# Involution stage: four row tiles for its kernel maps, sums and last convolution as 64x64 products

## The chip, the core and the metric

The kernel runs on one core of one Trainium2 chip. The engines are TensorE (PE, matrix products into PSUM; its weight loads are shown apart as PEld), VectorE (DVE), ScalarE (ACT), GpSimd (POOL) and SyncE (SP, which here only starts transfers). They run side by side and meet through semaphores. The metric is the device time of one execution in microseconds (us).

## What is computed

Eight blocks are applied in turn to 8 images of 64 channels and 16x16 pixels, in 32-bit floats. The change touches the seventh, the involution; its input is layer-normalised over the channels and its result is added to x:

```python
def conv1x1(x, w, b):
    return jnp.einsum('oc,bchw->bohw', w, x) + b[None, :, None, None]

def involution(x, w_red, b_red, w_span, b_span):
    kern = conv1x1(jax.nn.relu(conv1x1(x, w_red, b_red)), w_span, b_span)
    patches = extract_patches(x)        # the nine shifted copies, 3x3, zero padded
    return jnp.einsum('bkhw,bckhw->bchw', kern, patches)
x = dwconv3x3(x, w_in, b_in)            # depthwise, 3x3
x = involution(x, w_red, b_red, w_span, b_span)
x = dwconv3x3(x, w_out, b_out)          # depthwise, 3x3
```

`w_red` takes 64 channels to 16, `w_span` these to 9: one map per tap, the same for all channels.

## The kernel before

X is [128, 1024]: partitions are two halves of 64 channels (images 0-3 and 4-7), columns four images of 256 pixels. A half h of the columns is a pair of images (HC = 512 columns). Work is cut by h; the program of each engine is written out in order, and engines wait for each other by counting semaphores. Each block of the network is a Block of the program, at whose ends all engines meet.

In the involution's block (from L1636) the order is this. The layer norm (`ln_pe`, `ln_act`, `ln_dve`) ends in YP, a padded copy. The first depthwise convolution runs for h=0 on PE (nine products with diagonal matrices DGI of 128x128, L1674), placed in padded ZP by ACT (L1701), and for h=1 on DVE (L1723 to L1729). For each h, PE reduces ZP to 2x16 rows (L1678), ACT writes them into R with Relu (L1704), and row 32 of R is a row of ones that carries the bias of the maps. Then PE makes nine maps (L1684), each spread over the 64 channels of both halves, in PSUM banks 0 to 3 in turn. DVE multiplies each by the shifted window of ZP (L1740) and adds it to ACC (L1745), the last sum going to padded OP (L1743); a map's bank is free when its product is made (`k_used`). The last convolution of h=0 is nine products on PE (L1691). Of h=1, PE takes PTAPS = 4 taps and DVE the other five (L1747, L1749), which DVE adds to X (L1753); L1756 and L1758 add PE's parts from PSUM. DGI is made in the block before, by POOL. The next block begins with the layer norm of the last one (L153).

A product of 32-bit floats stands in the trace as two MATMUL records and two LDWEIGHTS records, one for each pass.

Of the kernel before, what the change touches and what calls it, by code (L numbers as in the profile page):

```python
# [11 lines left out]
ALU = mybir.AluOpType  # L12
# [47 lines left out]
    [("dwi", 9), ("dbi", 1), ("red", 32), ("bred", 1), ("span", 9 * P), ("dwo", 9), ("dbo", 1)],  # L60
# [12 lines left out]
def build(nc, x_dram, packs, idx_dram, out_dram):  # L73
    with ExitStack() as ctx:
# [1561 lines left out]
        with ExitStack() as sctx, nc.Block() as block:  # L1636
# [4 lines left out]
            M = sb("M7", [P, 2, HC], F32, sctx)  # L1641
            ACC = sb("ACC7", [P, COLS], F32, sctx)
            y_pad, pads, ones_set, z_ps, r_ps, r_in, k_ps, k_used, o_ready, o_ps = (sem("s7_" + n) for n in (
                "y_pad", "pads", "ones_set", "z_ps", "r_ps", "r_in", "k_ps", "k_used", "o_ready", "o_ps"))
            z_in = [sem(f"s7_z_in{h}") for h in range(2)]
            PTAPS = 4
            WROWS = PITCH + H
            WIN = sb("WIN", [P, WROWS, W], F32, sctx)

# [7 lines left out]
            @block.gpsimd  # L1657
            def _(pool):
                pool.memset(YP[:, :, :], 0.0).then_inc(y_pad, 1)
                for b in (ZP, OP):  # L1660
                    pool.memset(b[:, :, :], 0.0).then_inc(pads, 1)

                after_pool(pool, pool.memset(R[:, :], 0.0))
                pool.memset(R[32:33, :], 1.0).then_inc(ones_set, 1)

            @block.tensor
            def _(pe):
# [8 lines left out]
                for h in range(2):  # L1676
                    pe.wait_ge(z_in[h], 1)
                    pe.matmul(bank(6 + h)[0:32, :], wt("red"), pair(ZP, h, 2, 2), start=True, stop=True).then_inc(r_ps, 1)  # L1678
                    pe.wait_ge(r_in, h + 1)
                    for k in range(9):  # L1680
                        n = 9 * h + k
                        if n >= 4:
                            pe.wait_ge(k_used, n - 3)
                        pe.matmul(bank(n % 4), wt("span", k * P, P), R[:, h * HC:(h + 1) * HC],  # L1684
                                  start=True, stop=True).then_inc(k_ps, 1)

                for h in range(2):
                    pe.wait_ge(o_ready, h + 1)
                    taps = 9 if h == 0 else PTAPS
                    for m in range(taps):  # L1690
                        mm = pe.matmul(bank(4 + h), DGI[:, 9 + m, :], pair(OP, h, 1 + m // 3, 1 + m % 3), start=(m == 0), stop=(m == taps - 1))  # L1691
                    mm.then_inc(o_ps, 1)

            @block.scalar
            def _(act):
# [3 lines left out]
                act.wait_ge(ones_set, 1)  # L1699
                act.wait_ge(z_ps, 1)  # L1700
                act.activation(pair(ZP, 0, 2, 2), images(bank(4)), ACT.Identity, bias=wt("dbi")).then_inc(z_in[0], 1)  # L1701
                for h in range(2):
                    act.wait_ge(r_ps, h + 1)
                    act.activation(R[0:32, h * HC:(h + 1) * HC], bank(6 + h)[0:32, :], ACT.Relu, bias=wt("bred", 0, 1, 0, 32)).then_inc(r_in, 1)  # L1704


# [6 lines left out]
            def _(dve):  # L1713
# [19 lines left out]
                for h in range(2):  # L1733
                    dve.wait_ge(z_in[h], 1)
                    for k in range(9):
                        n = 9 * h + k
                        c = slice(h * HC, (h + 1) * HC)
                        dve.wait_ge(k_ps, n + 1)
                        o = ACC[:, c] if k == 0 else M[:, n % 2, :]
                        dve.tensor_tensor(images(o), images(bank(n % 4)), pair(ZP, h, 1 + k // 3, 1 + k % 3), ALU.mult).then_inc(k_used, 1)  # L1740
                        dve.wait_ge(k_used, n + 1)
                        if k == 8:
                            dve.tensor_tensor(pair(OP, h, 2, 2), images(ACC[:, c]), images(M[:, n % 2, :]), ALU.add).then_inc(o_ready, 1)  # L1743
                        elif k:
# [432 lines left out]
```

## Time and profile before

| | us |
|---|---|
| median of 3 runs | 609.9 (608.07 to 611.87) |
| the profiled execution | 609.04 |
| its span | 607.3 |
| PE, DVE, ACT, POOL busy | 513.8, 365.2, 293.1, 142.8 |
| involution block, from L153 at 454.11 to the last write of X at 505.03 | 50.92 |
| of it, from the first map at 472.25 | 32.78 |

The span runs from the first to the last instruction of the profiled execution; its own time has 1.7 us more around it. In a row of the timeline "x6" means six instructions merged into one line, from the start of the first to the end of the last; the bracket behind it is the time that the engine stood idle before, and what ended it. Sizes of PE rows are weight rows * columns, then the moving operand.

### The profile page before, as it was taken

To read this page: it belongs to the slowest core of one execution; us is meant where nothing else is said; L and a number is where in the kernel's file an instruction comes from. 1 tells how busy PE (TensorE), PEld (TensorE's weight loads), DVE (VectorE), ACT (ScalarE), POOL (GpSimd) and SP (SyncE) were. 2 spreads that over 40 slices of the span, in tenths; PEclk is the share of its full clock that TensorE was granted. 3 is DMA by queue.
4 is the path that set the end of the run, shared out by engine and by line. 5 is a ranking of instruction groups with operands and counts; after the bars stand their busy time and mean duration, and the time that the engine had idled before them with its cause. 6 is when DMAs were issued, how large, how long until landed. Compare 5 with 4: busy or idle time off the path is not lost. (4 is left out here: it accounts for less than half of the span.)

```text
span 607.3 us, 11742 instructions
## 1 busy us (share of the span) xinstructions
PE 513.8 (85%) x4973; PEld 263.1 (43%) x4973; DVE 365.2 (60%) x587; ACT 293.1 (48%) x393; POOL 142.8 (24%) x136
## 2 busy tenths in 40 slices
PE   3899989878998996788888788749997898999994
PEld 1334324543224966777687442313323334433231
DVE  2377994673554559878869257561437796633534
ACT  2573225255531159999998356635551102344230
POOL 8070000010011005888878300042002002000000
PEclk9999999998998999899899889868999999999998
DMA  7000000020000035455452000110002000000000
GB/s 251 1 2 2 2 1 1 1 102 0 1 16 16 2 104 206 160 184 195 176 177 74 1 19 0 49 42 0 1 13 101 0 1 1 1 0 1 3 15 17
DMA packets 7988, 29.42 MB, mean 48 GB/s; under 512 B 864, under 2 KB 2176, under 8 KB 7552
## 3 DMA queue, kind: packets, MB, share of 16 engines
q1 hardware_dynamic: 7936, 28.67, 14.1%
q8 instruction: 39, 0.64, 0.4%
q14 instruction: 13, 0.11, 0.1%
HBM read 28.00 MB, written 0.67 MB: 47 GB/s over the span
## 5 line engine op out<-in xcount | busy, mean ns | idle before, releaser
L1073 PE MATMUL PS<-GX,OH 128*128 128x64 f16 x2304 | 73.6, 195 | 19.1 <-DVE OH L1237 9.5
L1073 PEld LDWEIGHTS PS<-GX,OH 128*128 128x128 f16 x2304 | 71.0, 99 | 24.1 <-issue 12.7
L1162 ACT ACTIVATE DIST<-BC,wbuf 128x2048 f16<-128x2048 f16 x24 | 48.0, 2000 | 3.1 <-DMA BC<-idx_dram 1.4
L1969 DVE TENSOR_SCALAR HID<-PS,wbuf 128x512 f32<-128x512 f32 x32 | 23.8, 750 | 41.6 <-PE PS L1862 41.6
L1165 ACT ACTIVATE OH<-DIST 128x2048 f16<-128x2048 f16 x24 | 45.9, 1911 | 0.8
L1237 DVE TENSOR_SCALAR OH<-BC,wbuf 128x2048 f16<-128x2048 f16 x48 | 43.8, 935 | 2.6 <-DMA BC<-idx_dram 2.6
L1008 POOL TENSOR_TENSOR V<-SQ 128x512 f32<-128x512 f32 x18 | 27.9, 1547 | 57.5 <-DVE SQ L1248 56.7
L1908 ACT ACTIVATE HID<-PS,wbuf 128x512 f32<-128x512 f32 x32 | 22.0, 687 | 37.1 <-PE PS L1862 37.1
L692 DVE SCALAR_TENSOR_TENSOR D<-QKVP,wbuf,D 128x1024 f32<-128x1024 f32 x27 | 34.6, 1281 | 7.7 <-ACT D L592 6.9
L181 ACT ACTIVATE SQ<-PS 128x512 f32<-128x512 f32 x16 | 9.6, 597 | 60.9 <-PE PS L153 52.7
L153 PE MATMUL PS<-X,wconst 128*128 128x512 f32 x32 | 19.2, 731 | 22.9 <-DMA wconst<-pack_dram 8.6
L1858 PE MATMUL PS<-Y,wbuf 64*128 64x512 f32 x128 | 36.6, 615 | 2.3 <-DVE HID L1969 2.3
L423 PE MATMUL PS<-T,DG 128*32 128x512 f32 x336 | 37.1, 594 | 0.0
L1011 POOL TENSOR_TENSOR VAL<-V 128x256 f32<-128x256 f32 x36 | 35.9, 997 | 2.8
L1248 DVE TENSOR_TENSOR SQ<-PS,WC 128x512 f32<-128x512 f32 x36 | 23.1, 683 | 14.7 <-PE PS L1073 13.3
L921 DVE TENSOR_TENSOR HS<-PS,HID 128x512 f32<-128x512 f32 x32 | 20.6, 685 | 18.5 <-PE PS L806 18.4
L1870 PE MATMUL PS<-HID,wbuf 128*64 128x512 f32 x128 | 30.8, 604 | 0.0
L1008 POOL TENSOR_TENSOR V<-SD 128x512 f32<-128x512 f32 x18 | 26.7, 1485 | 4.8 <-DVE SD L1248 3.8
L873 ACT ACTIVATE HID<-PS,wbuf 128x512 f32<-128x512 f32 x32 | 20.1, 682 | 13.2 <-PE PS L797 13.1
L1248 DVE TENSOR_TENSOR SD<-PS,WC 128x512 f32<-128x512 f32 x36 | 23.1, 681 | 5.6 <-PE PS L1073 3.3
L1628 DVE TENSOR_TENSOR H2W<-H,WB 128x512 f32<-128x512 f32 x16 | 10.5, 689 | 24.7 <-ACT H L1569 12.5
L592 ACT ACTIVATE D<-PS,wbuf 128x512 f32<-128x512 f32 x12 | 8.3, 689 | 28.6 <-PE PS L423 28.6
(309 smaller groups left out, 931.0 us busy)
## 6 DMA issues: line engine op xcount, KB each, us to landing
BC<-idx_dram SPq DMA_DIRECT2D x36, 512.0 KB, 4.2
wbuf<-pack_dram SPq DMA_DIRECT2D x1, 1913.0 KB, 10.2
wbuf<-pack_dram SPq DMA_DIRECT2D x1, 1656.0 KB, 6.8
wbuf<-pack_dram SPq DMA_DIRECT2D x1, 1494.5 KB, 6.1
wbuf<-pack_dram SPq DMA_DIRECT2D x1, 820.0 KB, 11.7
wbuf<-pack_dram SPq DMA_DIRECT2D x1, 732.0 KB, 4.2
wbuf<-pack_dram SPq DMA_DIRECT2D x1, 602.5 KB, 3.4
X<-x_dram SPq DMA_DIRECT2D x2, 256.0 KB, 4.2
```

The source lines that it names most:

```text
L423: mm = pe.matmul(bank(DBANK[t % 2] + n)[32 * q:32 * q + 32, :], DG[:, (2 * j + hf) * NBLK + i, :], src, start=(i == blocks[0]), stop=(i == ...
L692: ins = dve.scalar_tensor_tensor(out=d, in0=window(QKVP[j], dy, dx), scalar=wt("dw5", j * 25 + 5 * dy + dx, 1), in1=d, op0=ALU.mult, op1=A ...
L1008: after_pool(pool, pool.tensor_tensor(V1[:, :, :, :], U[s % 2][:, :, 0:2, :], U[s % 2][:, :, 2:4, :], ALU.add))
L1011: pool.tensor_tensor(VAL[:, (s // 8) % 2, :, s % 8, :], V1[:, :, 0, :], V1[:, :, 1, :], ALU.add).then_inc(val_ready, 1)
L1073: mm = pe.matmul(o, OH[:, s % NOH, qh, t * P:(t + 1) * P], src, start=(qh == 0 and part == 0), stop=(qh == 1 and part == 1))
L1162: after_act(act, act.activation(DIST[:, :], BC[:, s % NBC, :], ACT.Abs, bias=wt("negq1")))
L1165: act.activation(OH[:, s % NOH, 1, :], DIST[:, :], ACT.Relu, bias=1.0, scale=-1.0).then_inc(scalar_oh, 1)
L1237: ins = dve.tensor_scalar(OH[:, s % NOH, qh, :], BC[:, s % NBC, :], wt("qidx", qh, 1), None, ALU.is_equal)
L1248: ins = dve.tensor_tensor(o, src, w, ALU.mult)
L1858: pe.matmul(bank(2 + (n + bh) % 4), wt("w1_3", e * FH3 + m * P, P, r, r + C), Y[r:r + C, bp * HC:(bp + 1) * HC], start=True, stop=False, t ...
L1870: pe.matmul(bank(bp)[C * bh:C * bh + C, :], wt("w2_3", (2 * e + m) * C, C), HID[:, (n + i) % 8, :], start=(e == 0 and m == 0), stop=False) ...
L1969: dve.tensor_scalar(HID[:, n % 8, :], bank(2 + n % 4), wt("b1_3", 2 * e + m, 1), 0.0, ALU.add, ALU.max).then_inc(hid_in_v, 1)
```

## The change

The work of the involution is cut by u, the first or second image of a pair, with both pairs side by side, n = 9u + k. R now holds four copies of the reduced rows (four products of 32 columns in four column tiles), and the weights `span` stand four times too, so that map n uses row tile n % 4 and bank n % 4. The bias of the maps has columns of its own, `bspan`. ACT evicts every map to KM (six buffers), DVE only multiplies (six buffers M), and PE sums the nine products of a u with unit matrices of 64x64: rows from one partition half g, output partitions by pair h, so each M buffer gives four products of 256 columns into two banks. `place` on ACT writes a sum from two banks to OP. The last convolution uses 64x64 blocks of DGI in the same four tiles and brings the images back to their places; DVE adds each u to X.

```diff
-    [("dwi", 9), ("dbi", 1), ("red", 32), ("bred", 1), ("span", 9 * P), ("dwo", 9), ("dbo", 1)],
+    [("dwi", 9), ("dbi", 1), ("red", 32), ("bred", 1), ("span", 9 * P), ("bspan", 9), ("dwo", 9), ("dbo", 1)],
...
-            M = sb("M7", [P, 2, HC], F32, sctx)
-            ACC = sb("ACC7", [P, COLS], F32, sctx)
-            y_pad, pads, ones_set, z_ps, r_ps, r_in, k_ps, k_used, o_ready, o_ps = (sem("s7_" + n) for n in (
-                "y_pad", "pads", "ones_set", "z_ps", "r_ps", "r_in", "k_ps", "k_used", "o_ready", "o_ps"))
+            NK, NM = 6, 6
+            KM = sb("KM7", [P, NK, HC], F32, sctx)
+            M = sb("M7", [P, NM, HC], F32, sctx)
+            y_pad, pads, z_ps, r_ps, r_in, k_ps, k_in, m_ready, m_used, o_in, o_ps = (sem("s7_" + n) for n in (
+                "y_pad", "pads", "z_ps", "r_ps", "r_in", "k_ps", "k_in", "m_ready", "m_used", "o_in", "o_ps"))
             z_in = [sem(f"s7_z_in{h}") for h in range(2)]
-            PTAPS = 4
+            NP = 18
+            ABANK, OBANK = (4, 6), (4, 0)
...
+            def of_pairs(pad, u, dy, dx):
+                base = min(dy, 2)
+                at = u * PITCH + dy - base
+                v = pad[:, base:base + 4 * PITCH, dx:dx + W].rearrange("p (h r) w -> p h r w", h=2)
+                return v[:, :, at:at + H, :]
+            def two_banks(n):
+                return PS[:, n * 512:(n + 2) * 512].rearrange("p (k c) -> p k c", k=2)[:, :, 0:PIX]
...
-                after_pool(pool, pool.memset(R[:, :], 0.0))
-                pool.memset(R[32:33, :], 1.0).then_inc(ones_set, 1)
...
-                for h in range(2):
+                for h in (1, 0):
                     pe.wait_ge(z_in[h], 1)
-                    pe.matmul(bank(6 + h)[0:32, :], wt("red"), pair(ZP, h, 2, 2), start=True, stop=True).then_inc(r_ps, 1)
-                    pe.wait_ge(r_in, h + 1)
-                    for k in range(9):
-                        n = 9 * h + k
-                        if n >= 4:
-                            pe.wait_ge(k_used, n - 3)
-                        pe.matmul(bank(n % 4), wt("span", k * P, P), R[:, h * HC:(h + 1) * HC],
-                                  start=True, stop=True).then_inc(k_ps, 1)
-                for h in range(2):
-                    pe.wait_ge(o_ready, h + 1)
-                    taps = 9 if h == 0 else PTAPS
-                    for m in range(taps):
-                        mm = pe.matmul(bank(4 + h), DGI[:, 9 + m, :], pair(OP, h, 1 + m // 3, 1 + m % 3), start=(m == 0), stop=(m == taps - 1))
-                    mm.then_inc(o_ps, 1)
+                    for q in range(4):
+                        mm = pe.matmul(bank(6 + h)[32 * q:32 * q + 32, :], wt("red"), pair(ZP, h, 2, 2), start=True, stop=True,
+                                       tile_position=(0, 32 * q))
+                    mm.then_inc(r_ps, 1)
+                def maps(i):
+                    for q in range(min(4, NP - 4 * i)):
+                        n, r = 4 * i + q, 32 * q
+                        u, k = n // 9, n % 9
+                        if i:
+                            pe.wait_ge(k_in, n - 3)
+                        rhs = R[r:r + 32, :].rearrange("p (h v x) -> p h v x", h=2, v=2)[:, :, u, :]
+                        pe.matmul(bank(q), wt("span", k * P, P, r, r + 32), rhs, start=True, stop=True, tile_position=(r, 0)).then_inc(k_ps, 1)
+                def add(n):
+                    u, k = n // 9, n % 9
+                    pe.wait_ge(m_ready, n + 1)
+                    for h in range(2):
+                        for g in range(2):
+                            a = C * g
+                            mm = pe.matmul(bank(ABANK[u] + g, PIX)[C * h:C * h + C, :], wt("ident", a, C, a, a + C),
+                                           M[a:a + C, n % NM, h * PIX:(h + 1) * PIX], start=(k == 0), stop=(k == 8), tile_position=(a, C * h))
+                    mm.then_inc(m_used, 1)
+                def out_tap(u, m):
+                    if m == 0:
+                        pe.wait_ge(o_in, u + 1)
+                    for g in range(2):
+                        for h in range(2):
+                            a = C * h
+                            r0 = (2 * g + u) * PITCH + 1 + m // 3
+                            mm = pe.matmul(bank(OBANK[u] + h, PIX)[C * g:C * g + C, :], DGI[a:a + C, 9 + m, a:a + C],
+                                           OP[a:a + C, r0:r0 + H, 1 + m % 3:1 + m % 3 + W], start=(m == 0), stop=(m == 8), tile_position=(a, C * g))
+                    if m == 8:
+                        mm.then_inc(o_ps, 1)
+                pe.wait_ge(r_in, 2)
+                maps(0)
+                maps(1)
+                for n in range(4):
+                    add(n)
+                maps(2)
+                for n in range(4, 8):
+                    add(n)
+                maps(3)
+                for n in range(8, 12):
+                    add(n)
+                maps(4)
+                taps = {12: (0,), 13: (1,), 14: (2, 3), 15: (4,), 16: (5,), 17: (6, 7, 8)}
+                for n in range(12, NP):
+                    add(n)
+                    for m in taps[n]:
+                        out_tap(0, m)
+                for m in range(9):
+                    out_tap(1, m)
...
-                act.wait_ge(ones_set, 1)
                 act.wait_ge(z_ps, 1)
                 act.activation(pair(ZP, 0, 2, 2), images(bank(4)), ACT.Identity, bias=wt("dbi")).then_inc(z_in[0], 1)
-                for h in range(2):
-                    act.wait_ge(r_ps, h + 1)
-                    act.activation(R[0:32, h * HC:(h + 1) * HC], bank(6 + h)[0:32, :], ACT.Relu, bias=wt("bred", 0, 1, 0, 32)).then_inc(r_in, 1)
+                for i, h in enumerate((1, 0)):
+                    act.wait_ge(r_ps, i + 1)
+                    act.activation(R[:, h * HC:(h + 1) * HC], bank(6 + h), ACT.Relu, bias=wt("bred")).then_inc(r_in, 1)
+                def place(u):
+                    act.wait_ge(m_used, 9 * u + 9)
+                    act.activation(of_pairs(OP, u, 2, 2), two_banks(ABANK[u]).rearrange("p k (r w) -> p k r w", w=W), ACT.Copy).then_inc(o_in, 1)
+                for n in range(NP):
+                    act.wait_ge(k_ps, n + 1)
+                    if n >= NK:
+                        act.wait_ge(m_ready, n - NK + 1)
+                    act.activation(KM[:, n % NK, :], bank(n % 4), ACT.Identity, bias=wt("bspan", n % 9, 1)).then_inc(k_in, 1)
+                    if n == 13:
+                        place(0)
+                place(1)
...
-                for h in range(2):
-                    dve.wait_ge(z_in[h], 1)
-                    for k in range(9):
-                        n = 9 * h + k
-                        c = slice(h * HC, (h + 1) * HC)
-                        dve.wait_ge(k_ps, n + 1)
-                        o = ACC[:, c] if k == 0 else M[:, n % 2, :]
-                        dve.tensor_tensor(images(o), images(bank(n % 4)), pair(ZP, h, 1 + k // 3, 1 + k % 3), ALU.mult).then_inc(k_used, 1)
-                        dve.wait_ge(k_used, n + 1)
-                        if k == 8:
-                            dve.tensor_tensor(pair(OP, h, 2, 2), images(ACC[:, c]), images(M[:, n % 2, :]), ALU.add).then_inc(o_ready, 1)
-                        elif k:
-                            after(dve, dve.tensor_tensor(ACC[:, c], ACC[:, c], M[:, n % 2, :], ALU.add))
-                dve.wait_ge(o_ready, 2)
-                after(dve, dve.tensor_scalar(WIN[:, :, :], window(OP, PTAPS), wt("dwo", PTAPS, 1), wt("dbo"), ALU.mult, ALU.add))
-                for m in range(PTAPS + 1, 9):
-                    after(dve, dve.scalar_tensor_tensor(out=WIN[:, :, :], in0=window(OP, m), scalar=wt("dwo", m, 1), in1=WIN[:, :, :],
-                                                        op0=ALU.mult, op1=ALU.add))
-                for i in range(2):
-                    x = X[:, HC + i * PIX:HC + (i + 1) * PIX].rearrange("p (r w) -> p r w", w=W)
-                    ins = dve.tensor_tensor(x, x, WIN[:, i * PITCH:i * PITCH + H, :], ALU.add)
-                after(dve, ins)
-                dve.wait_ge(o_ps, 1)
-                dve.scalar_tensor_tensor(out=X[:, 0:HC], in0=bank(4), scalar=wt("dbo"), in1=X[:, 0:HC], op0=ALU.add, op1=ALU.add)
-                dve.wait_ge(o_ps, 2)
-                dve.tensor_tensor(X[:, HC:COLS], bank(5), X[:, HC:COLS], ALU.add)
+                dve.wait_ge(z_in[0], 1)
+                for n in range(NP):
+                    u, k = n // 9, n % 9
+                    dve.wait_ge(k_in, n + 1)
+                    if n >= NM:
+                        dve.wait_ge(m_used, n - NM + 1)
+                    if n == 0:
+                        dve.wait_ge(z_in[1], 1)
+                    maps = KM[:, n % NK, :].rearrange("p (h r w) -> p h r w", h=2, r=H)
+                    dve.tensor_tensor(M[:, n % NM, :].rearrange("p (h r w) -> p h r w", h=2, r=H), maps,
+                                      of_pairs(ZP, u, 1 + k // 3, 1 + k % 3), ALU.mult).then_inc(m_ready, 1)
+                for u in range(2):
+                    dve.wait_ge(o_ps, u + 1)
+                    x = X[:, :].rearrange("p (h v c) -> p h v c", h=2, v=2)[:, :, u, :]
+                    dve.scalar_tensor_tensor(out=x, in0=two_banks(OBANK[u]), scalar=wt("dbo"), in1=x, op0=ALU.add, op1=ALU.add)
...
+    for q in range(4):
+        for g in range(2):
+            r = 32 * q + 16 * g
+            put("bred", v["L3_conv_b_red"][:, None], r)
+            for k in range(9):
+                put("span", np.broadcast_to(v["L3_conv_w_span"][k][:, None], (16, C)), r, k * P + C * g)
+    rows("bspan", v["L3_conv_b_span"])
```

The next rows list PE's instructions in its order (line, kind, output and inputs, size of the output, how many). First the place where the maps begin, before: the reduction by half (L1678), the maps (L1684), the last convolution (L1691).

```order
L1674 MATMUL PS<-YP,DGI 128x512 x9
L1678 MATMUL PS<-ZP,wbuf 32x512
L1684 MATMUL PS<-R,wbuf 128x512 x9
L1678 MATMUL PS<-ZP,wbuf 32x512
L1684 MATMUL PS<-R,wbuf 128x512 x9
L1691 MATMUL PS<-OP,DGI 128x512 x13
```

The same place in the changed kernel, as far as the fourth group of maps (L1688 reduces, L1700 makes maps, L1709 sums products).

```order
L1683 MATMUL PS<-YP,DGI 128x512 x9
L1688 MATMUL PS<-ZP,wbuf 32x512 x8
L1700 MATMUL PS<-R,wbuf 128x512 x8
L1709 MATMUL PS<-M,wconst 64x256 x16
L1700 MATMUL PS<-R,wbuf 128x512 x4
L1709 MATMUL PS<-M,wconst 64x256 x16
L1700 MATMUL PS<-R,wbuf 128x512 x4
L1709 MATMUL PS<-M,wconst 64x256 x16
L1700 MATMUL PS<-R,wbuf 128x512 x2
```

Maps now come in groups, with the sums of four earlier products between two groups. The end of the stage on PE in the changed kernel follows, from sum 15 on (L1721 is the last convolution, four products to a tap).

```order
L1709 MATMUL PS<-M,wconst 64x256 x4
L1721 MATMUL PS<-OP,DGI 64x256 x4
L1709 MATMUL PS<-M,wconst 64x256 x4
L1721 MATMUL PS<-OP,DGI 64x256 x4
L1709 MATMUL PS<-M,wconst 64x256 x4
L1721 MATMUL PS<-OP,DGI 64x256 x48
```

The 48 are the last three taps of u=0 and all nine of u=1. On DVE the whole stage behind the first convolution was a run of products and additions with taps at its end; here are its first and last rows before (with a line left out between), which the change's two rows below replace.

```order
-L1740 TENSOR_TENSOR ACC<-PS,ZP 128x512
-L1740 TENSOR_TENSOR M<-PS,ZP 128x512
-L1745 TENSOR_TENSOR ACC<-ACC,M 128x512
...
-L1743 TENSOR_TENSOR OP<-ACC,M 128x2x16x16
-L1747 TENSOR_SCALAR WIN<-OP,wbuf 128x544
-L1749 SCALAR_TENSOR_TENSOR WIN<-OP,wbuf,WIN 128x544 x4
-L1753 TENSOR_TENSOR X<-X,WIN 128x256 x2
-L1756 SCALAR_TENSOR_TENSOR X<-PS,wbuf,X 128x512
-L1758 TENSOR_TENSOR X<-PS,X 128x512
...
+L1805 TENSOR_TENSOR M<-KM,ZP 128x512 x18
+L1810 SCALAR_TENSOR_TENSOR X<-PS,wbuf,X 128x2x256 x2
```

Eighteen products and two additions are left on DVE.

## Rows read from the trace of the kernel before

**Rows 1.** Busy time by stretch; columns as in the first line.
```profile
core 0: us, PE busy (x) PEld busy (x) DVE busy (x) ACT busy (x) POOL busy (x), PEclk, DMA share, GB/s
472.25:482.30 10.05, 9.26 (x20) 3.39 (x20) 8.30 (x12) 0.69 (x2) 0.00 (x0) 1.00 0.00 0
482.30:492.60 10.30, 9.16 (x18) 3.11 (x19) 9.83 (x15) 1.02 (x2) 0.00 (x0) 1.00 0.00 0
492.60:504.40 11.80, 11.70 (x27) 4.70 (x25) 10.55 (x17) 0.00 (x0) 0.00 (x0) 1.00 0.01 1
```
**Rows 2.** Timeline, start of the stage: start, length, engine, line, operation [idle before].
```profile
469.66 0.70 ACT L1701 ACTIVATE ZP<-PS,wbuf 128x512 f32<-128x512 f32 x1 [12.05 <-PE PS L1674]
470.42 1.07 PE L1678 MATMUL PS<-ZP,wbuf 128*32 128x512 f32 x2 [0.87 <-ACT ZP L1701]
471.52 0.68 ACT L1704 ACTIVATE R<-PS,wbuf 32x512 f32<-32x512 f32 x1 [1.16 <-PE PS L1678]
472.25 8.31 PE L1684 MATMUL PS<-R,wbuf 128*128 128x512 f32 x18 [0.77 <-ACT R L1704]
473.49 0.69 DVE L1740 TENSOR_TENSOR ACC<-PS,ZP 128x512 f32<-128x512 f32 x1 [4.94 <-PE PS L1684]
```
**Rows 3.** Groups by line in 454 to 515: busy, mean ns | idle before.
```profile
L1740 DVE TENSOR_TENSOR M<-PS,ZP 128x512 f32<-128x512 f32 x16 | 11.1, 691 | 0.7 <-PE PS L1684 0.2
L1745 DVE TENSOR_TENSOR ACC<-ACC,M 128x512 f32<-128x512 f32 x14 | 9.7, 691 | 0.5
L1743 DVE TENSOR_TENSOR OP<-ACC,M 128x512 f32<-128x512 f32 x2 | 1.4, 692 | 0.1
```
**Rows 4.** Timeline, end of the stage on DVE.
```profile
497.42 0.69 DVE L1743 TENSOR_TENSOR OP<-ACC,M 128x512 f32<-128x512 f32 x1
498.15 0.56 DVE L1747 TENSOR_SCALAR WIN<-OP,wbuf 128x544 f32<-128x544 f32 x1
498.75 3.25 DVE L1749 SCALAR_TENSOR_TENSOR WIN<-OP,wbuf,WIN 128x544 f32<-128x544 f32 x4
502.03 0.76 DVE L1753 TENSOR_TENSOR X<-X,WIN 128x256 f32<-128x256 f32 x2
502.83 0.75 DVE L1756 SCALAR_TENSOR_TENSOR X<-PS,wbuf,X 128x512 f32<-128x512 f32 x1
504.34 0.69 DVE L1758 TENSOR_TENSOR X<-PS,X 128x512 f32<-128x512 f32 x1 [0.76 <-PE PS L1691]
```
**Rows 5.** Groups by line in 454 to 515, the last convolution on PE.
```profile
L1691 PE MATMUL PS<-OP,DGI 128*128 128x512 f32 x26 | 11.7, 604 | 0.0
```
**Rows 6.** Timeline of DVE and ACT where six independent operations follow each other.
```profile
427.03 3.70 DVE L1628 TENSOR_TENSOR H2W<-H,WB 128x512 f32<-128x512 f32 x6 [12.24 <-ACT WB L1592]
132.09 3.75 ACT L873 ACTIVATE HID<-PS,wbuf 128x512 f32<-128x512 f32 x6
```
**Rows 7.** Timeline of PE: 256 columns without tiles, then 64x64 tiles; L1533's mean; L1684's min/median/max ns.
```profile
425.26 1.89 PE L1533 MATMUL PS<-WT,SEL 128*128 128x256 f32 x8
116.55 2.81 PE L526 MATMUL PS<-ATT,wbuf 64*64 64x512 f32 x24
L1533 PE MATMUL PS<-WT,SEL 128*128 128x256 f32 x8 | 1.9, 379 | 0.0
L1684 PE MATMUL PS<-R,wbuf x36: 592/593/697, 472.3 to 492.2; 128*128 128x512 f32 x36
```
**Rows 8.** The chain that ended last, in order of time: start, length, what.
```profile
577.36 1.87 PE PS L1870 x8
579.23 1.06 PE PS L1858 x4
580.29 0.22 PE PS L1862 x2
580.50 0.86 PE PS L1858 x4
581.36 0.22 PE PS L1862 x2
581.58 1.87 PE PS L1870 x8
```
**Rows 9.** Busy time by stretch, columns as in rows 1: PE's clock.
```profile
183.40:186.80 3.40, 1.27 (x20) 0.86 (x24) 3.24 (x7) 0.87 (x2) 1.27 (x2) 1.00 0.00 0
186.80:190.20 3.40, 3.40 (x20) 1.28 (x16) 1.29 (x3) 0.00 (x0) 0.00 (x0) 0.51 0.02 5
469.60:473.00 3.40, 1.81 (x4) 0.62 (x5) 0.00 (x0) 1.38 (x2) 0.00 (x0) 1.00 0.00 0
```

More of the change, by code:

```diff
@@ L2135, in pack_weights @@
     diag2("red", v["L3_conv_w_red"].T, 0)
-    put("bred", v["L3_conv_b_red"][:, None], 0)
-    put("bred", v["L3_conv_b_red"][:, None], 16)
-    for k in range(9):
-        a = np.broadcast_to(v["L3_conv_w_span"][k][:, None], (16, C))
-        put("span", a, 0, k * P)
-        put("span", a, 16, k * P + C)
-        put("span", np.broadcast_to(v["L3_conv_b_span"][k:k + 1, None], (1, P)), 32, k * P)
+    for q in range(4):
[5 more added lines that the diff above has]
+    rows("bspan", v["L3_conv_b_span"])
     twice("dwo", v["L3_conv_w_out"].reshape(C, 9))
```

## The prediction, made before the changed kernel was run

> **What bounds the kernel now.** I first read the stretches of the involution stage [rows 1]. The stage's own body lies between 472.25, where the first kernel map is issued, and 505.03 us, where the last addition into X ends. In the three stretches between them DVE is busy 8.30 of 10.05, 9.83 of 10.30 and 10.55 of 11.80 us, ACT 0.69, 1.02 and 0.00, and TensorE runs at its upper level (granted clock 1.00, so 2.4 GHz) throughout. The timeline of the start [rows 2] shows a serial hand-over: ACT places ZP, PE reduces, ACT writes R, PE makes the first map at 472.25, and DVE starts its first product at 473.49. From there DVE is a chain: 18 products and 16 additions (14 + 2), each 691 or 692 ns [rows 3], and since each waits for the one before, two of them follow 0.72 us apart (473.49 and the last OP addition at 497.42: 33 steps of 0.725). Behind it, the timeline of the end [rows 4]: five taps on DVE, two additions, then the two that read PSUM, end 504.34 + 0.69 = 505.03. PE's 26 records at 604 ns [rows 5] lie beside this; they end only just behind DVE (a wait of 0.76). So DVE's chain of 31.5 us sets the stage, PE follows it within 0.8 us, and ACT is free.
>
> **What the change removes and adds.** DVE loses 16 additions, the five taps and three of the four closing steps; it keeps 18 products (now of two SBUF operands) and two closing additions of 0.75 us. ACT gains 18 evictions and 2 placements of OP. PE gains 18 sums, each a quad of 64x64 products with 256 columns, and its last convolution becomes 18 quads of the same shape (all nine taps of all images) where 13 full-array products of 512 columns stood. The maps shrink from 18 full-array products to five groups of up to four row tiles. POOL's memsets of R go; nothing waited for them. The start up to 472.25 stays: the reduction is now issued four times side by side, h=1 first, but h=0 still waits for the same ZP at 470.36.
>
> **Prices.** DVE: H2W's six independent products took 3.70 us, so one is 0.69 long and the next starts (3.70 - 0.69) / 5 = 0.60 later; ACT: six evictions with bias took 3.75 us, so 0.61 [rows 6]. A product is two records. A record of 512 columns takes 0.43 us of the array (four of L1858 on two tiles took 0.86 [rows 8]) and, at 0.59 long [rows 7], is readable about 0.16 later; one of 256 columns takes (1.89 - 0.38) / 7 = 0.216 [rows 7]. Do four 64x64 tiles run together? Yes: 24 records of 512 columns (6 quads of records, one per tile) took 2.81 us, that is (2.81 - 0.59) / 5 = 0.44 per four [rows 7]. No row has 64x64 with 256 columns. Bounds: 2 x 0.216 = 0.43 us for a quad of products if the four still run together, 0.86 if a quad took as long as one of 512 columns. I take 0.43 for the sums and 0.445 for the taps, whose operand is a padded window (11.70 us for 26 records is 0.444 each against 0.43 [rows 5, 8]); the weight loads, the only thing that could stretch a shorter product, did not stretch the 256-column row.
>
> Changing the tiling costs something. In the chain at the end of the program [rows 8] L1858 (64x128 tiles) takes 0.86 us in a row of its own tiling and 1.06 behind L1870 (128x64 tiles); L1870 takes 1.87 where four records' time in sequence, 4 x 0.43, is 1.72. So 0.20 into tiles with 128 columns of weights and 0.15 into tiles with 64, and the new tiling starts only when the old one has streamed out. The Trainium skill (TensorEngine Tiling (Array Packing), Key Properties) says that changing the mode drains TensorE, while other tiles of one mode work in parallel. By that rule every switch here is paid; without it the seven switches behind the first maps would cost nothing and the sum below would be 1.2 us smaller (4 x 0.15 + 3 x 0.20). The row agrees with the rule.
>
> **The new path, step by step** (PE's order: maps 0-3, 4-7, sums 0-3, maps 8-11, sums 4-7, maps 12-15, sums 8-11, maps 16-17, then sums and taps).
> - Maps 0-3 issue at 472.25, are readable at 473.36 (0.10 for the first load, 2 x 0.43, 0.16). ACT evicts them; evictions end at 474.05, 474.65, 475.25, 475.85. Maps 4-7 each wait for one of these (the bank), the last issues at 475.94 and streams to 476.90. This paced group is the one real bubble: DVE's products, 0.60 apart, hide behind it.
> - Sums 0-3: 0.15 + 4 x 0.43 = 1.88, to 478.78. Maps 8-11, all banks free: 0.20 + 0.86 = 1.06, to 479.84. Sums 4-7: 1.88, to 481.74.
> - ACT had waited for maps 8-11 (its eviction 7 ends at 478.3) and starts at 480.04; its evictions end every 0.60, the fourth at 482.5. Map 15 waits for that one, streams to 483.53. From the end of sums 4-7 that is 1.8 us where an unpaced group takes 1.06.
> - Sums 8-11: 1.88, to 485.41. Maps 16-17: 1.06, to 486.47. Then six sums with nine tap quads: 0.15 + 6 x 0.43 + 9 x 0.445 = 6.75, to 493.22; the products are all ready by 488.7 and PE waits for none.
> - Placement 1 follows sum 17 (491.9 + 0.16, 0.69 long: 492.8), just inside this; its cover is the three taps behind sum 17 (1.34 us against 1.0). Nine tap quads: 4.0, to 497.23. Readable at 497.4, DVE's last addition 0.75 long: 498.2; with 0.1 more at two hand-overs that wait, 498.4.
>
> 505.03 - 498.4 = 6.6 us gained. PE becomes the bound: about 20 us of array time in 25. The profiled execution took 609.04 us (span 607.3 and 1.7 around it); less 6.6 it is 602.4. The median shown is 609.9, 0.9 above it, which would give 603.3; I predict 602.8.
>
> **Rivals.**
> - *All overlaps better*: switches cheaper, or ACT's and PE's hand-overs in the third map group closed. With no switch cost at all 1.2 less, with the group of maps 12-15 unpaced 0.7 less: gain 8.5, 600.5 us. Against it: [rows 8]. Chance 0.15.
> - *ACT and DVE at the pace of a wait*: where each step waits, DVE's pitch was 0.72 in [rows 3]. Then the first paced group is 0.3 longer and map 15 0.3 later, placement 1 comes out from under its cover by some tenths: gain 5.5 to 6, 603.8 us. It is my forecast with its terms at their other end. Chance 0.22.
> - *The quads are slower than 0.43*, for example 0.5 because sixteen loads and products per quad have to be issued in it. 36 quads x 0.07 = 2.5 less: gain 4, 605.3 us. For it: no row of this shape; against: L526 and the 256-column row. Chance 0.12.
> - *Slower than before*: four tiles of 256 columns take what four of 512 take, 0.86. Each quad costs 0.43 more, of 36 quads some 34 on the path: 14.6 us more than forecast, so 8 us slower, 617 us. It turns the sign where a quad exceeds 0.43 + 6.6 / 34 = 0.62. Against it: four 512-column records took 0.44, no less than their columns, so nothing fixed is seen in them. Chance 0.05.
> - *The clock falls*: it fell behind a stretch in which PE was busy 1.27 of 3.40 us, in the middle of just such 64x64 work, while it held through 469.60:473.00 with 1.81 of 3.40 busy [rows 9]. The new start is as sparse there and the paced group after it uses one row tile at a time. At half clock a stretch of 3.4 us costs up to 1.7: gain 4.9, 604.5 us. It could also shift such a fall into or out of the next stage. Chance 0.11, in either half of it.
>
> **How the numbers follow.** The forecast itself has 0.35, its own range 601 to 605. Better 0.15, at 600.5; the pace 0.22, at 603.8; slow quads 0.12 at 605.3; the clock 0.11 at 604.5; slower 0.05. Three runs of before spread over 608.07 to 611.87, so the median of the new one moves by some 1.5 either way. Low is 599.5, a microsecond under the better case; high 608.0 takes in slow quads with a fall of the clock. Outside lie the slower case and a rest of each side, 0.15. About 1%, 6.1 us, is what a measurement of this kernel can tell from no change: faster by over 1% is below 603.8. The better case, most of the forecast and a third of the pace case lie there: 0.52. Within 1% come the rest: 0.40. Slower 0.08, of which 0.05 are slow quads and 0.03 unforeseen.
>
> **What would show it.** First map at 472.25 and first eviction near 473.4. Two records of a sum in 0.43 us, with all four tiles starting within some 20 ns. The sums' first records behind maps 0.1 us later than the drain. ACT idle before its evictions 8 and 12, DVE idle and no longer the bound. PE without waits from about 483 us to the end of the taps at 497.2. A gap before out_tap(1) would show that placement 1 has lost its cover; a first addition later than 497.4 by over 1 us would show that the quads' price was wrong. A clock below 1.00 between 470 and 498 would be the last rival.

## The result

| | before | changed |
|---|---|---|
| median of 11 runs, us | 610.07 (605.05 to 612.14) | 606.45 (603.52 to 609.07) |
| ratio | 1 | 0.9942, 95% interval 0.9918 to 0.9967 |
| span of the profiled execution | 607.3 | 605.8 |
| first map to last write of X | 32.78 | 29.15 |

The changed kernel is 3.6 us faster, 0.6%: within the range that was given, but only half of the forecast gain of 6.6 to 7.1 us. In the profiled execution the stage is 3.6 us shorter, while its start is 2.1 us later (first map at 474.36, not 472.25 as in [rows 2]), a difference that arises ahead of anything the diff touches. So spans and medians carry other parts of the program as well; below, the experiments are read by the stage's own time.

The timeline of the changed kernel shows where it runs and waits (start, length, engine, line, operation, and the idle time before). L1700 makes maps, L1709 sums, L1765 evicts, L1805 multiplies, L1721 is the last convolution.

```profile
474.36 1.14 PE L1700 MATMUL PS<-R,wbuf 32*128 32x512 f32 x8 [0.81 <-ACT R L1755]
475.52 4.87 ACT L1765 ACTIVATE KM<-PS,wbuf 128x512 f32<-128x512 f32 x8 [1.21 <-PE PS L1700]
476.26 3.41 PE L1700 MATMUL PS<-R,wbuf 32*128 32x512 f32 x8 [0.76 <-ACT KM L1765]
476.30 3.70 DVE L1805 TENSOR_TENSOR M<-KM,ZP 128x512 f32<-128x512 f32 x6 [5.71 <-ACT KM L1765]
479.60 3.69 PE L1709 MATMUL PS<-M,wconst 64*64 64x256 f32 x32
483.22 2.09 PE L1700 MATMUL PS<-R,wbuf 32*128 32x512 f32 x8
485.24 1.96 PE L1709 MATMUL PS<-M,wconst 64*64 64x256 f32 x32
485.32 2.42 ACT L1765 ACTIVATE KM<-PS,wbuf 128x512 f32<-128x512 f32 x4 [4.93 <-PE PS L1700]
497.11 5.57 PE L1721 MATMUL PS<-OP,DGI 64*64 64x256 f32 x96
502.76 0.75 DVE L1810 SCALAR_TENSOR_TENSOR X<-PS,wbuf,X 128x512 f32<-128x512 f32 x1 [3.29 <-PE PS L1721]
```

The same 32 records of four sums take 3.69 us at 479.60 and 1.96 at 485.24, and a group of four maps 2.09 in between against 1.14 at the start. The stretches say why (columns as in [rows 1]; the number behind POOL's is PE's granted clock):

```profile
core 0: us, PE busy (x) PEld busy (x) DVE busy (x) ACT busy (x) POOL busy (x), PEclk, DMA share, GB/s
474.40:478.90 4.50, 3.74 (x16) 1.44 (x16) 2.60 (x5) 3.38 (x6) 0.00 (x0) 0.95 0.00 0
478.90:485.70 6.80, 6.80 (x49) 2.66 (x52) 2.49 (x4) 1.84 (x4) 0.00 (x0) 0.53 0.01 2
485.70:503.50 17.80, 16.99 (x264) 10.69 (x256) 7.87 (x12) 7.98 (x14) 0.00 (x0) 1.00 0.01 2
```

For 6.8 us the array runs at its lower level, 1.2 GHz. The fall begins some 0.45 us ahead of the second row, which is why the first has 0.95 and the second 0.53, not 0.50. In the kernel before, the granted clock was 1.00 throughout the stage [rows 1]. Half of 6.8 is 3.4; 29.15 less 3.4 would be 25.8, and the forecast was 26.15 (498.4 - 472.25). That gave the theory for the experiments: **A**, the clock took the missing gain. Rival **B**: the fall was an accident of this execution, and a price or a wait of the new path is larger than predicted.

The groups by line of the stage (busy us, mean ns | idle before, and who ended it) show the change of the bound: DVE now stands idle ahead of its products for as long as it works on them, and the two lines of PE shown have no idle time.

```profile
L1805 DVE TENSOR_TENSOR M<-KM,ZP 128x512 f32<-128x512 f32 x18 | 11.5, 688 | 11.8 <-ACT KM L1765 10.8 <-PE PS L1709 1.0
L1709 PE MATMUL PS<-M,wconst 64*64 64x256 f32 x144 | 11.4, 438 | 0.0
L1765 ACT ACTIVATE KM<-PS,wbuf 128x512 f32<-128x512 f32 x18 | 11.1, 692 | 7.3 <-PE PS L1700 7.2
L1721 PE MATMUL PS<-OP,DGI 64*64 64x256 f32 x144 | 9.2, 382 | 0.0
```

### The profile page after: what moved, and what is told of

The parts are those of the page before. It is cut to its first block and busy times, and to the rows that moved or that the text cites. A ratio compares the mean times of both kernels' runs of the same rounds, so it can differ in the third digit from the quotient of the medians.

```text
span 605.8 us, 12285 instructions
## 1 busy us (share of the span) xinstructions
PE 515.4 (85%) x5243; PEld 269.8 (45%) x5247; DVE 349.2 (58%) x564; ACT 305.5 (50%) x413; POOL 141.1 (23%) x134
## 5 line engine op out<-in xcount | busy, mean ns | idle before, releaser
L1073 PE MATMUL PS<-GX,OH 128*128 128x64 f16 x2304 | 75.2, 196 | 19.1 <-DVE OH L1237 8.7
L1073 PEld LDWEIGHTS PS<-GX,OH 128*128 128x128 f16 x2304 | 72.5, 100 | 24.3 <-DVE OH L1237 12.5
L1008 POOL TENSOR_TENSOR V<-SQ 128x512 f32<-128x512 f32 x18 | 27.6, 1531 | 60.2 <-DVE SQ L1248 59.3
L1628 DVE TENSOR_TENSOR H2W<-H,WB 128x512 f32<-128x512 f32 x16 | 10.5, 690 | 24.2 <-ACT H L1569 12.5
```

Of the source, the lines that this page charges most:

```text
L1008: after_pool(pool, pool.tensor_tensor(V1[:, :, :, :], U[s % 2][:, :, 0:2, :], U[s % 2][:, :, 2:4, :], ALU.add))
L1073: mm = pe.matmul(o, OH[:, s % NOH, qh, t * P:(t + 1) * P], src, start=(qh == 0 and part == 0), stop=(qh == 1 and part == 1))
```

## The experiments

All compute the same result; "fill" is `keep_busy`, a helper that the kernel before has already: full-array bf16 products of 512 columns that nobody reads, 12 of them in 2.76 us. The table gives for every profiled execution the stage's time, the stretch at the lower clock within it, and the time from the last write of X to the end; then the median and the ratio to the kernel before, run beside it.

| kernel | stage | low in it | behind it | median | ratio (95%) |
|---|---|---|---|---|---|
| before | 32.78 | 0 | 102.2 | 610.07 | |
| changed | 29.15 | 6.8 | 102.3 | 606.45 | 0.9942 (0.9918 to 0.9967) |
| after_again | 27.54 | 3.4 | 104.0 | 607.37 | 0.994 (0.9915 to 0.9965) |
| e_group | 27.57 | 3.4 | 103.9 | 605.96 | 0.9937 (0.991 to 0.9965) |
| e_fill_early | 27.55 | 3.4 | 103.9 | 607.75 | 0.9965 (0.9936 to 0.9993) |
| e_fill_late | 26.09 | 0 | 102.3 | 602.68 | 0.9871 (0.9834 to 0.9908) |
| e_fill | 26.06 | 0 | 102.3 | 603.33 | 0.988 (0.9842 to 0.9918) |
| fill_again | 26.06 | 0 | 102.3 | 602.74 | 0.9877 (0.9844 to 0.991) |
| e_fullmaps | 26.76 | 0 | 102.3 | 603.12 | 0.9888 (0.9848 to 0.9927) |
| e_switch | 27.18 | 0 | 103.9 | 606.15 | 0.9928 (0.99 to 0.9956) |
| e_pairs | 25.03 | 0 | 103.9 | 603.61 | 0.9892 (0.9864 to 0.992) |
| e_banks | 24.25 | 0 | 103.9 | 603.03 | 0.989 (0.9858 to 0.9921) |
| e_banks_nofill | 24.27 | 0 | 104.0 | 602.23 | 0.9874 (0.9839 to 0.9909) |
| e_banks_last | 24.24 | 0 | 102.2 | 601.92 | 0.9852 (0.9819 to 0.9885) |

Add the columns "stage" and "behind it": from the first map to the end the kernel before took 135.0 us, the four executions with a fall in the stage 131.5 each, and the three filled ones (e_fill, e_fill_late, fill_again) 128.3 to 128.4. A fall of 6.8 us in the stage, or one of 3.4 there and another of 3.4 behind it (the rows with 103.9 and 104.0 are those with this second fall), come to the same 3.1 us. This is most of the 4.0 between the medians of after_again and e_fill, and 135.0 - 131.5 = 3.5 fits the 3.6 of the result.

### The changed kernel again

> The changed kernel once more, beside the experiments. Theory A (the clock): TensorE's granted clock falls to about 0.5 shortly behind the paced maps 4-7 and stays there for some 6.8 us; the stage from the first map to the last write of X takes about 29.2 us, as in the first execution. Theory B (the fall was an accident of that execution, and what is missing of the gain is a wait or a price of its own): the clock holds here, and the stage still takes 28 us or more. If the clock holds and the stage takes about 26 us, the prices of the prediction were right and the fall comes and goes.

The clock fell again at the same place, for 3.4 us only, and the stage took 27.54 where 29.2 was expected: the time goes with the length of the fall. (The second row begins some 0.35 us late, as in the rows above.)

```profile
472.90:477.60 4.70, 3.91 (x16) 1.48 (x16) 2.74 (x5) 3.51 (x7) 0.00 (x0) 0.96 0.00 0
477.60:481.00 3.40, 3.40 (x33) 1.74 (x32) 2.35 (x4) 1.23 (x3) 0.00 (x0) 0.55 0.03 5
```

### Filling PE's gaps ahead of the first sums

```diff
+                keep_busy(pe, 5, 3)
                 pe.wait_ge(r_in, 2)
                 maps(0)
+                keep_busy(pe, 5, 12)
                 maps(1)
...
-                        if i:
+                        if i == 1:
+                            pe.wait_ge(k_in, 4)
+                        elif i:
                             pe.wait_ge(k_in, n - 3)
```

> Maps 4-7 are issued together behind the fourth eviction, and PE's two idle places ahead of them hold products that nobody reads: 3 of 512 bf16 columns while R is written, 12 between maps 0-3 and maps 4-7. The result is unchanged. Theory A: the clock stays at 1.00 through the stage, which takes 26.0 to 26.6 us (29.15 less half of the 6.8 us at the lower clock is 25.8, and the fill may delay a map by 0.3); the median is about 3 us below that of the changed kernel. Theory B: the stage stays at 28 to 29 us, since no price of its own is touched.

The filled kernel's timeline: the 12 products, the grouped maps 4-7, then four sums in 1.96 us at once.

```profile
473.83 1.14 PE L1702 MATMUL PS<-R,wbuf 32*128 32x512 f32 x8
474.90 2.76 PE L149 MATMUL PS<-wconst 128*128 128x512 bf16 x12
477.60 1.14 PE L1702 MATMUL PS<-R,wbuf 32*128 32x512 f32 x8
478.67 1.96 PE L1711 MATMUL PS<-M,wconst 64*64 64x256 f32 x32
480.55 1.80 PE L1702 MATMUL PS<-R,wbuf 32*128 32x512 f32 x8
```

The stage took 26.06 us, 6.7 less than before, with no other price touched: theory A. The median is 4.0 us below that of after_again, run beside it (603.33 and 607.37); B's 28 to 29 did not come. Run once more later:

> The filled kernel again, beside the two above: clock 1.00 through the stage, 26.0 to 26.2 us, median near 603.3. If the clock falls here, the fill only makes the fall rarer.

It took 26.06 again.

### The grouping alone, and maps 4-7 on the full array

> Maps 4-7 are issued together behind the fourth eviction, without the fill: a control for the fill. Theory A: PE now stands idle for about 2.7 us where it ran one row tile at a time, the clock falls at the same place or earlier, and the stage takes 29 to 30 us. Theory B: the grouping itself, which gives the same readiness of map 7, changes nothing: within 0.3 us of the changed kernel. If this control holds the clock, the paced row tiles and not the sparse work are what matters.

> Maps 4-7 use the full array (all four copies of R and of the weights, and ACT evicts them with a scale of 0.25), still each behind its eviction; everything else as in the changed kernel. It tells whether PE's idle gaps or its work in one row tile at a time bring the clock down. Theory A in its form 'single row tiles': the clock holds at 1.00, maps 4-7 take 3.6 us in place of 2.7, the stage takes about 27 us. Theory A in its form 'gaps': the gaps ahead are as before, the clock falls all the same, about 30 us. Theory B: about 30 us with any clock.

e_group is the first diff without the two `keep_busy` lines. e_fullmaps is the changed kernel with

```diff
+                        if i == 1:
+                            rhs = R[:, :].rearrange("p (h v x) -> p h v x", h=2, v=2)[:, :, u, :]
+                            pe.matmul(bank(q), wt("span", k * P, P), rhs, start=True, stop=True).then_inc(k_ps, 1)
+                            continue
```

and a scale of 0.25 in ACT's eviction of these four maps. The first two rows are e_group's, around its fall; the next ones are those of e_fullmaps, one kernel to a fence.

```profile
471.00:474.90 3.90, 1.40 (x12) 0.58 (x16) 1.96 (x4) 2.42 (x4) 0.00 (x0) 1.00 0.00 0
474.90:478.30 3.40, 3.40 (x28) 1.34 (x28) 1.79 (x4) 1.98 (x4) 0.00 (x0) 0.53 0.02 5
```

```profile
475.28 3.70 PE L1702 MATMUL PS<-R,wbuf 128*128 128x512 f32 x8 [0.76 <-ACT KM L1769]
473.40:478.90 5.50, 4.74 (x16) 1.72 (x16) 3.59 (x6) 4.27 (x7) 0.00 (x0) 1.00 0.00 0
478.90:485.00 6.10, 6.10 (x81) 3.24 (x80) 3.73 (x7) 3.20 (x6) 0.00 (x0) 1.00 0.01 3
```

The control fell as expected: grouping is not what helped (27.57, below the expected 29 to 30 because the fall was of 3.4 us). e_fullmaps kept the clock with the gaps of the changed kernel left as they were (0.81 and 0.76 ahead of its two groups of maps), at the price of the longer maps: 26.76 against 26.06. So the gaps of 0.81 and 0.76 alone do not bring it down. What stood there when it fell was single 32-row tiles, one after another, in place of the full array, or a gap of 2.49 us as in e_group. Two things are left open: e_fullmaps was profiled once (its median, 603.12 against 607.37, speaks for the same in its other runs), and its maps differ in two ways, four times the rows and a group that runs 3.7 us on end in place of some 2.7, which this run does not tell apart.

### Which of the two fills

> Only the fill of 12 products between maps 0-3 and maps 4-7, which stand grouped. Theory A, the time ahead of the fall is the paced group of maps 4-7 alone: the clock holds, stage 26.0 to 26.4 us. Rival: the reduction and the wait for R matter as well: the clock falls for one stretch of 3.4 us, stage about 27.6.

> Only 3 products while PE waits for R; maps 4-7 paced as in the changed kernel. Theory A: the clock falls about 4 us behind the first map, as without the fill, stage 27.5 to 29.2 us. Rival (the gap ahead of the first map is what brings it down): the clock holds and the stage takes 26.0 to 26.4 us.

The late one alone does all of it, 26.09; the early one nothing, 27.55. Around the early one's fall:

```profile
474.50:479.00 4.50, 3.74 (x16) 1.46 (x16) 2.58 (x5) 3.36 (x6) 0.00 (x0) 0.99 0.00 0
479.00:482.40 3.40, 3.40 (x33) 1.79 (x32) 2.50 (x4) 1.37 (x3) 0.00 (x0) 0.51 0.02 5
```

### The price of a change of the tiling

```diff
                 for n in range(12, NP):
                     add(n)
+                    if n >= 14:
+                        at = AT["ident"][1]
+                        pe.matmul(bank(2, 8), wconst[:, at:at + 64].bitcast(BF16), wconst[:, at:at + 4].bitcast(BF16), start=True, stop=True)
```

> The filled kernel with four tiny full-array products (8 bf16 columns, nobody reads them) put behind the sums of products 14 to 17, where PE never waits: each changes the tiling away from 64x64 and back. If a change of the tiling costs what the prediction took (0.15 into 64x64, as much into the full array, after the old one has streamed out), the stage grows by 4 x 0.3 = 1.2 us, to 27.3, less where the last of them hides beside the second placement. If products of different tilings could overlap, it grows by less than 0.2.

```profile
488.40 0.61 PE L1711 MATMUL PS<-M,wconst 64*64 64x256 f32 x8
488.83 0.63 PE L1723 MATMUL PS<-OP,DGI 64*64 64x256 f32 x8
489.28 0.61 PE L1711 MATMUL PS<-M,wconst 64*64 64x256 f32 x8
489.83 0.18 PE L1747 MATMUL PS<-wconst 128*128 128x8 bf16 x1
489.94 1.12 PE L1723 MATMUL PS<-OP,DGI 64*64 64x256 f32 x16
```

A tap follows its sum 0.43 us later (488.40, 488.83); with a tiny full-array product between, 0.66 later (489.28, 489.94), and the small product itself starts 0.12 behind the end of the sum's 0.43. The stage grew by 27.18 - 26.06 = 1.12 us, 0.28 for each small product with its two changes, of which this gap is 0.23. That agrees with the 0.15 that the prediction took for each change, and here products of different tilings did not overlap.

### Fewer sums on PE

Four pairs of products of the second image are added on DVE, and PE sums five times instead of nine:

```diff
+                    if n - 1 in HALF:
+                        after(dve, ins)
+                        ins = dve.tensor_tensor(M[:, n % NM, :], M[:, n % NM, :], M[:, (n - 1) % NM, :], ALU.add)
+                    ins.then_inc(m_ready, 1)
```

with `HALF = (10, 12, 14, 16)`, no `add` for these on PE, and the taps behind sums 13, 15 and 17, three each.

> The filled kernel, and for the second image of each pair DVE adds products 10 and 11, 12 and 13, 14 and 15, 16 and 17 to each other, so that PE sums five times in place of nine. If PE is the bound from the middle of the stage on, as its row without idle time says, the stage loses 4 x 0.43 = 1.7 us, to 24.3 us, less what ACT's and DVE's hand-overs take back; the median falls to about 601.8. If DVE or ACT sets it, nothing changes or the stage grows by the four additions' 0.7 us each.

```profile
486.55 0.66 PE L1714 MATMUL PS<-M,wconst 64*64 64x256 f32 x8 [0.30 <-DVE M L1816]
487.03 1.54 PE L1726 MATMUL PS<-OP,DGI 64*64 64x256 f32 x24
487.74 0.69 DVE L1816 TENSOR_TENSOR M<-M 128x512 f32<-128x512 f32 x1
488.48 0.66 PE L1714 MATMUL PS<-M,wconst 64*64 64x256 f32 x8
489.66 0.69 DVE L1816 TENSOR_TENSOR M<-M 128x512 f32<-128x512 f32 x1
490.41 0.66 PE L1714 MATMUL PS<-M,wconst 64*64 64x256 f32 x8
```

25.03: 1.03 of the 1.7 us. A pair on DVE takes 1.92 us from addition to addition (487.74, 489.66), PE's sum with three taps 0.43 + 3 x 0.445 = 1.77, so PE now follows DVE. Its wait of 0.30 us at 486.55 and two rounds of 1.93 in place of 1.77 (486.55, 488.48, 490.41) are 0.6 of the 0.7 us of gain that is missing.

### Seven maps at once

Maps go to banks 0 to 6 and on to 7, 0, 1, ... so that PE is ahead of ACT; the order is maps 0-6, 7-10, sums 0-3, maps 11-14, sums 4-7, maps 15-17, then ten sums with the taps. M has eight buffers. The core of the diff against the changed kernel:

```diff
+                BANK = (0, 1, 2, 3, 4, 5, 6, 7, 0, 1, 2, 3, 6, 7, 0, 1, 2, 3)
+                FREE = {8: 3, 9: 3, 10: 3, 11: 4, 12: 7, 13: 8, 14: 9, 15: 10, 16: 11, 17: 12}
...
+                maps(range(0, 7))
+                keep_busy(pe, 7, 5)
+                maps(range(7, 11))
```

> A version meant to be faster: seven maps are issued at once into seven PSUM banks, 5 products that nobody reads fill the eighth until ACT has evicted three, then maps 7-10, sums 0-3, maps 11-14, sums 4-7, maps 15-17, and the ten last sums with the taps; M has eight buffers. If what is left of the stage is PE's work and the bubble behind maps 0-3, the stage takes 24.3 to 24.8 us against 26.06 of the filled kernel, the clock holding at 1.00. If ACT's or DVE's hand-overs set the pace, it stays at 25.5 or more.

> The same without the 5 filling products. Theory A (the clock comes down behind sparse work of single row tiles and gaps): the gap of about 1.2 us behind seven maps that ran four at a time is shorter than before, so the clock holds and the stage is that of e_banks within 0.2 us; if the fall comes all the same, the stage is 1.5 us longer.

Without the fill:

```profile
472.02 1.99 PE L1705 MATMUL PS<-R,wbuf 32*128 32x512 f32 x14 [0.81 <-ACT R L1759]
473.18 6.47 ACT L1769 ACTIVATE KM<-PS,wbuf 128x512 f32<-128x512 f32 x11 [1.21 <-PE PS L1705]
473.96 9.21 DVE L1809 TENSOR_TENSOR M<-KM,ZP 128x512 f32<-128x512 f32 x15 [5.71 <-ACT KM L1769]
475.08 1.14 PE L1705 MATMUL PS<-R,wbuf 32*128 32x512 f32 x8 [1.06 <-ACT KM L1769]
476.91 1.96 PE L1716 MATMUL PS<-M,wconst 64*64 64x256 f32 x32 [0.69 <-ACT KM L1769]
```

Both took 24.3 us in the stage, 1.8 less than the filled kernel, so PE's bubbles were worth what they had seemed, and the clock held with a gap of 1.06 us as well. But the medians are those of the filled kernel. The column "behind it" shows why in the traces: 103.9 and 104.0 where the filled kernel has 102.3. There the clock fell in the next stage, behind a wait of PE for DVE, which was still finishing the first half of the output. The wait, then the stretches around the fall, both without the fill:

```profile
567.30 0.69 PE L1914 MATMUL PS<-Y,wbuf 64*128 64x512 f32 x1 [1.49 <-DVE HID L2025]
```

```profile
565.60:569.00 3.40, 1.91 (x7) 0.66 (x8) 2.60 (x5) 0.61 (x2) 0.00 (x0) 0.95 0.26 60
569.00:572.40 3.40, 3.40 (x10) 0.76 (x8) 0.43 (x1) 0.16 (x1) 0.00 (x0) 0.55 0.10 22
```

The wait is not enough for a fall. The kernel before has the same one, and its time behind the stage is 102.2, without a fall:

```profile
576.02 0.69 PE L1858 MATMUL PS<-Y,wbuf 64*128 64x512 f32 x1 [1.49 <-DVE HID L1969]
```

Over the profiles, the later fall stands where the stage took 24.2 to 25.0 or 27.2 to 27.6 us, and not at 26.1 to 26.8, 29.15 or 32.78 (the next run, with a fill there, apart). So it goes with the length of the stage ahead of it; no run shows why.

### The next stage's gap

```diff
                     for bh in range(2):
+                        if n == 46 and bh:
+                            keep_busy(pe, 6, 6)
                         if n >= 4:
                             pe.wait_ge((hid_in_a, hid_in_v)[bh], n // 2 - 1)
```

> The version with seven maps at once and no fill in the involution stage, and 6 products that nobody reads in the next stage, where PE waits 1.49 us for DVE's finish(0). In the profiles taken so far the time behind the involution stage was either 102.2 to 102.3 us or 103.8 to 104.0, the latter wherever the clock fell for 3.4 us near that wait. If that fall is what gave back the stage's gain of 1.7 us in the medians, the part behind the stage takes 102.3 us, the span is near 598.5 and the median about 600.7. If it is something else, the part stays near 103.9 and the median near 602.2.

```profile
570.06 1.24 PE L149 MATMUL PS<-wconst 128*128 128x512 bf16 x5 [0.16 <-issue]
566.00:572.00 6.00, 5.74 (x24) 1.96 (x24) 5.83 (x10) 1.31 (x2) 0.00 (x0) 1.00 0.01 3
572.00:576.00 4.00, 4.00 (x19) 1.30 (x19) 0.81 (x3) 0.77 (x2) 0.00 (x0) 1.00 0.29 66
```

The row has five of the six products. Behind the stage 102.2 us, as expected, and the clock at 1.00. The span did not come down to 598.5: it was 602.6, because the stage began at 476.2, later than in any other execution. The granted clock of its first 130 us was 0.97, where the kernel before had 1.00, but fill_again had 0.97 there too and its stage began at 472.26, so what delayed the start is open. The median, 601.92, is the lowest of all, 0.9852 of the kernel before, but not the 600.7 expected, and its interval overlaps those of the filled kernels. That the gap's fall is what the medians of e_banks carried is therefore shown in one trace and not by the medians.

## Why the prediction was wrong

**The bound and the prices held.** DVE's chain went, PE became the bound, and the new path without a fall of the clock, with maps 4-7 grouped behind a fill, took 26.06 us in three profiled executions within 0.03 (e_fill, e_fill_late, fill_again), where the steps gave 26.15. The changed order itself was never seen with the clock up all through. Four sums took 1.96 as a row of the timeline, which is 1.88 and the tail that merges into the next. Four 64x64 tiles of 256 columns run together: the eight records of a sum take 0.43 us, the lower bound; the rival of 0.86 is out, and so is that of 0.5. Maps 0-3 readable 1.16 us after their issue (475.52), predicted 1.11. Placement 1 stayed under its cover of three taps: the taps run on without a gap.

**The step that failed** is the one that left the clock at its upper level in the forecast and gave its fall a chance of 0.11 and a price of "up to 1.7". The clock fell in the stage in all four profiled executions that had neither the late fill nor full-array or seven-deep maps, each time 4.1 to 4.5 us behind the first map; in the first of them for 6.8 us, twice the stretch that I had priced. The prices by stage times are 27.55 - 26.06 = 1.5 us for 3.4 and 29.15 - 26.06 = 3.1 for 6.8, a little under half of the stretch. The filled kernel is itself late by a little: its sums begin 4.84 us behind the first map (473.83, 478.67), where the steps have 4.65, so each price may be up to 0.2 higher, which is half. With the second fall, which three of the four have behind the stage, all four lost 3.1 us against the filled kernels, and the median lay 3.65 above the forecast of 602.8. The prediction said that such a fall could also be shifted into the next stage, but gave that no price. I had compared the start of the stage before, which held with PE busy 1.81 of 3.40 [rows 9], and named the paced single row tiles as a risk, but counted them as busy time. The row of the changed kernel says 3.74 of 4.50 busy, more than that start, and the clock fell all the same. The busy share of a row does not tell what those products are; here each of the four maps used one 32-row tile.

The Trainium skill (TensorE: Matmul & The Clock Gate, Why this matters for your kernels) advises against idle gaps of PE between bursts of products, and means longer ones than any here. In these traces the clock fell behind a gap of 2.49 us in e_group and behind gaps of 0.81 and 0.76 in the changed kernel, while e_fullmaps held with the same two. So for this kernel the measurement decides, and the advice was not enough.

**A slip without effect**: the prediction says that three of DVE's four closing steps go and two stay; it is two and two.

**The range** held the median, but its upper part was meant for slow quads together with a fall; a fall alone was put at 604.5, 2 us under the 606.45 measured. **The other rivals**: the pace of a wait did not appear (ACT's eight evictions took 4.87 us, 0.60 apart). The better case, closing the paced groups, was reachable, but only by another order of the maps.

**Open**: how often the clock falls for 6.8, for 3.4 or not at all in a kernel's unprofiled runs. Also open are why the sparse start brings the clock down, beyond what e_fullmaps and e_group tell, and why the later fall goes with the length of the stage. The stage's start lay between 469.7 and 476.2 over the fourteen profiles, so a single span says little. Each kernel but the changed and the filled one was profiled once.

## What to carry to other kernels

When work is moved from the full array into small tiles that each wait for another engine, look at what PE does in the first microseconds of the new order, not at its busy share: here, behind paced single row tiles, the fall of the clock took back 1.5 to 3.1 us in the stage, of a gain of 6.7. Groups of four did not help by themselves (e_group); seven maps at once, as deep as the free banks allowed, did, and so did products that nobody reads in the gap. Then read the granted clock of the stretches behind it. A gain of a microsecond or two in one stage may be hidden in the median by a fall in another.

## What the runs showed of the hardware

- The clock came down to the lower level at the end of 4.5 us in which PE was busy 3.74, and stayed up in e_banks_nofill where it was busy 3.13 of the first 4.90 us:

```profile
472.00:476.90 4.90, 3.13 (x22) 1.04 (x23) 2.94 (x5) 3.72 (x7) 0.00 (x0) 1.00 0.00 0
```

- A full-array product of 8 columns between 64x64 quads cost 0.28 us, the two changes of the tiling included (e_switch).
- A quad of 64x64 products with 256 columns, eight MATMUL and eight LDWEIGHTS records, takes 0.43 us (e_switch, 488.40 to 488.83).
- A stretch at the lower clock cost the stage about half of its length, where PE was the bound: 3.1 us for 6.8, 1.5 for 3.4.
